# A graph kernel's front stages joined: degrees from self-loop ranks, x scaled during the edge sort; one stage split, one stage's gate banks doubled

## The chip, the cores and the metric

The kernel runs on 1 core of one Trainium2 chip. A NeuronCore has TensorE (PE, matmuls), VectorE (DVE), ScalarE (ACT), GpSimd (POOL), SyncE (SP, which here only issues DMAs) and 16 DMA engines. The metric is the device time of the whole program in microseconds (us), the median of several runs.

## The reference

Four layers of graph networks run one after the other on 50000 nodes with 128 features each. The 100000 edges come sorted by destination: 50000 random ones and one self loop per node. `deg` counts the edges of a node without its own loop.

```python
src = jnp.concatenate([_s, _d, _loop]); dst = jnp.concatenate([_d, _s, _loop])
_o = jnp.argsort(dst, stable=True); src = src[_o]; dst = dst[_o]

def gcn_layer(x, edge_index, W, b, num_nodes):        # layer 0, used twice; it adds self loops once more
    deg = jax.ops.segment_sum(jnp.ones_like(dst), dst, num_segments=num_nodes)
    dinv = jnp.where(deg > 0, jax.lax.rsqrt(deg), 0.0)
    norm = dinv[src] * dinv[dst]
    return jax.ops.segment_sum((x @ W)[src] * norm[:, None], dst, num_segments=num_nodes) + b

def sage(h, w_self, w_neigh, b):                      # layer 1, used three times
    agg = jax.ops.segment_sum(h[src], dst, num_segments=n) * inv_deg
    return h @ w_self + agg @ w_neigh + b
```

Layer 2 weighs messages by a sigmoid of source and destination and puts them through a gated recurrent unit (two gates and a candidate) with a batch norm; layer 3 is one more neighbour and self product. Between them stand residuals and layer norms.

## The kernel before, in words

Nodes lie in T = 98 groups of 512 (4 blocks of 128 partitions). The program is a chain of stages, each closed by a barrier of all engines: `sort_edges` (L301), `fold_weights` (L2110), `count_degrees` (L1000), `scale_degrees` (L1067), `scale_x` (L1128), `gcn_first` (L1167), `gcn_second`, `sage_first` (L1373), `sage_second`, `sage_third`, `attend` (L1747), two batch-norm stages and `combine`. Behind some of them stands `if_general`, a branch for inputs that don't have the expected form; it isn't taken here.

**Sort.** It takes 100000 edges as 782 columns of 128, drops the self loops and packs the other edges into 425 slots (17 for each 4 groups). VectorE works out a partition (`spot`) and a slot for every edge, builds one-hot matrices `parts` (L555, 8 columns an operation, 98 operations) and values (L547, L549), and TensorE multiplies the two to place source and destination (L413), 8 columns a round. The loads of all weights run beside it (L385).

**Degrees.** `count_degrees` builds another set of one-hots from the sorted edges (L1028, L1035) and sums them on TensorE (L1052), which gives the degree of every node; the table goes to memory. `scale_degrees` reads it back and makes 1/sqrt(deg + 1) (`dinv_n`) and 1/deg (`inv_n`), by groups of nodes and as rows in memory. `scale_x` loads x group by group (L773), multiplies it by `dinv_n` on ACT, 4 operations a group (L1150), and stores it as `t_x0` (L777).

**Stages over groups.** `over_groups` (L125) runs each engine's steps over the 98 groups with a fixed lag per step. In a stage that sums over edges, VectorE copies the indices of a group (`aim`, L642), GpSimd issues 3 to 5 indirect gathers of 128 rows (L649), VectorE builds one-hots (L677), and TensorE sums 5 or 7 pieces a group (`sum_by_feature`, L713). With `split=True` ACT first takes the rows' high part (`take_hi`, L672) and VectorE the low part (`take_lo`, L684), both in a narrower float32 form that TensorE multiplies in one pass each; without it a float32 matmul takes two passes, and the rows buffer has two rings instead of one. `gcn_first` and `sage_second` are split, `sage_first` isn't.

**attend.** Per group TensorE computes two gates into banks 3 and 4 (L1821, L1822) and the candidate's parts into banks 5 and 6 (L1824, L1825). It first waits for `opened` (ACT has read the gates of the group before) and `mixed` (VectorE has read banks 5 and 6, L1897 and L1900).

## Time and profile before

| what | us |
|---|---|
| median of 3 runs (5885.31 to 5894.61) | 5894.18 |
| the profiled execution | 5898.03 |
| its span, first to last instruction | 5896.2 |
| TensorE busy | 4786.1 (81%) |
| VectorE busy | 3866.7 (66%) |
| GpSimd busy | 2984.4 (51%) |
| ScalarE busy | 2695.8 (46%) |

How to read the rows below. A row of the table by stretch gives the stretch from the start of the span, its length, then busy time and number of instructions of PE, PEld (weight loads), DVE, ACT and POOL, the share of TensorE's clock that was granted, the busy share of the DMA engines and GB/s. A row by line gives line, engine, operation, what is written from what, the shapes (partitions x elements), the count, then busy us in all, mean ns of one, and the engine's idle time before them with what ended it. A timeline row gives start and duration in us; "x14" means that 14 instructions are merged. A float32 matmul that isn't split leaves two records, one per pass. Matmuls overlap: the distance from start to start is shorter than one's duration.

### The profile page before, as it was taken

Reading aid. Unit: us, or ns where it says so; the run is one execution under the profiler, and the core shown is the slowest. Engines: PE = TensorE matmul, PEld = TensorE weight load, DVE = VectorE, ACT = ScalarE, POOL = GpSimd, SP = SyncE. Lnnn points to the kernel's source line nnn. Section 1 sums busy time; section 2 is a strip of 40 time slices with the busy share of each in tenths; the row PEclk is TensorE's granted clock in tenths of the full one; section 3 lists DMA queues with packets and bytes.
Section 4 is the critical chain, followed back from the end, with each engine's and each line's share of the span. In section 5 each row is a group of like instructions: output and inputs, shape, how many; then the busy total and the mean of one; then the engine's idle time right before and its main releaser. Section 6 shows DMA issues by size and latency. Waiting matters only on the chain. (4 is left out here: it accounts for less than half of the span.)

```text
span 5896.2 us, 104499 instructions
## 1 busy us (share of the span) xinstructions
PE 4786.1 (81%) x27114; PEld 3751.8 (64%) x27114; DVE 3866.7 (66%) x11812; ACT 2695.8 (46%) x6502; POOL 2984.4 (51%) x2957
## 2 busy tenths in 40 slices
PE   2207999666599998999999998778699999546887
PEld 1106888555488886777777776677565666326777
DVE  9905777576666664555555554788577777786666
ACT  0074444465622222222222222677566666694455
POOL 0007776677677754343433432777555555005776
PEclk9999999777799998999999998999899999657999
DMA  1097998445467764444444443777655555595554
GB/s 31 6 326 222 274 274 270 144 147 145 144 207 226 224 208 151 149 155 146 155 149 149 155 147 102 186 199 198 185 164 155 161 159 156 178 305 158 148 151 139
DMA packets 523170, 1024.15 MB, mean 174 GB/s; under 512 B 107887, under 2 KB 115094, under 8 KB 519962
## 3 DMA queue, kind: packets, MB, share of 16 engines
q1 hardware_dynamic: 423194, 803.47, 41.2%
q0 software_dynamic: 99840, 219.14, 16.2%
q8 instruction: 52, 0.85, 0.1%
q14 instruction: 84, 0.69, 0.0%
HBM read 686.75 MB, written 335.49 MB: 173 GB/s over the span
## 5 line engine op out<-in xcount | busy, mean ns | idle before, releaser
L649 POOL DMA_INDIRECT s_rows<-t_h,s_index x416 | 526.5, 1266 | 854.9 <-DVE s_index L642 753.5
L649 POOL DMA_INDIRECT g_rows<-t_x,g_index x416 | 415.3, 998 | 594.9 <-DVE g_index L642 485.5
L649 POOL DMA_INDIRECT at_rows<-t_m,at_index x416 | 433.6, 1042 | 407.1 <-DVE at_index L642 302.4
L649 POOL DMA_INDIRECT cb_rows<-t_x,cb_index x416 | 397.9, 956 | 465.5 <-DVE cb_index L642 342.7
L713 PE MATMUL bank<-s_onehot,s_rows 128*128 128x80 f32 (+9 forms) x2344 | 475.3, 356 | 129.4 <-DMA s_rows<-t_v,s_index 93.0
L713 PEld LDWEIGHTS bank<-s_onehot,s_rows 128*128 128x128 f32 x2344 | 407.9, 203 | 190.0 <-DVE s_onehot L677 52.1
L649 POOL DMA_INDIRECT s_rows<-t_v,s_index x416 | 400.9, 964 | 211.5 <-issue 124.1
L649 POOL DMA_INDIRECT s_rows<-t_x,s_index x416 | 403.4, 970 | 179.3 <-issue 121.4
L649 POOL DMA_INDIRECT g_rows<-t_h,g_index x416 | 402.3, 967 | 172.1 <-issue 124.7
L713 PE MATMUL bank<-g_onehot,g_rows 128*128 128x80 f32 (+9 forms) x1172 | 299.2, 420 | 196.8 <-DMA g_rows<-t_h,g_index 192.2
L1599 DVE TENSOR_TENSOR s_rout<-bank,s_x 128x512 f32<-128x512 f32 x98 | 67.8, 692 | 587.2 <-PE bank L1543 587.2
L713 PEld LDWEIGHTS bank<-g_onehot,g_rows 128*128 128x128 f32 x1172 | 248.9, 243 | 251.8 <-issue 156.6
L1543 PEld LDWEIGHTS bank<-wuv_s,s_hid 128*128 128x128 f32 x3136 | 365.5, 192 | 47.4 <-issue 47.4
L677 DVE TENSOR_SCALAR s_onehot<-iota,dcol 128x224 f32<-128x224 f32 (+15 forms) x1248 | 386.0, 371 | 0.6
L1566 ACT ACTIVATE s_hid<-bank,sb_c 128x512 f32<-128x512 f32 x196 | 124.1, 684 | 569.0 <-PE bank L1531 569.0
L1531 PE MATMUL bank<-s_ht,ws_s 128*128 128x512 f32 x784 | 369.5, 594 | 0.0
L1531 PE MATMUL bank<-s_agg,wn_s 128*128 128x512 f32 x784 | 368.4, 592 | 0.0
L1543 PE MATMUL bank<-wuv_s,s_hid 128*128 128x128 f32 x3136 | 366.0, 275 | 0.9 <-DVE s_rout L1599 0.9
L713 PE MATMUL bank<-g_onehot,g_hi 128*128 128x112 f32 (+9 forms) x586 | 178.1, 340 | 180.4 <-DVE g_lo L684 171.5
L713 PE MATMUL bank<-cb_onehot,cb_rows 128*128 128x80 f32 (+9 forms) x1172 | 242.0, 360 | 91.3 <-DMA cb_rows<-t_x,cb_index 76.5
L713 PE MATMUL bank<-s_onehot,s_hi 128*128 128x80 f32 (+9 forms) x1172 | 288.4, 287 | 22.1 <-DVE s_lo L684 18.1
L713 PE MATMUL bank<-s_onehot,s_lo 128*128 128x80 f32 (+9 forms) x1172 | 285.0, 285 | 0.0
(308 smaller groups left out, 12601.2 us busy)
## 6 DMA issues: line engine op xcount, KB each, us to landing
s_scale<-inv_d SPq DMA_DIRECT2D x196, 256.0 KB
t_h<-s_hout SPq DMA_DIRECT2D x98, 512.0 KB
s_own<-t_h SPq DMA_DIRECT2D x98, 512.0 KB
t_m<-s_mout SPq DMA_DIRECT2D x98, 264.0 KB
at_own<-t_m SPq DMA_DIRECT2D x98, 264.0 KB
t_x<-sx_out SPq DMA_DIRECT2D x98, 256.0 KB
g_own<-t_x SPq DMA_DIRECT2D x98, 256.0 KB
g_scale<-dinv_d SPq DMA_DIRECT2D x98, 256.0 KB
```

The costliest lines, as they stand in the source:

```text
L649: pool.indirect_dma_start(out=self.rows[:, self.ring(q) + k, :], out_offset=None, in_=self.table[0:NPAD, :], in_offset=bass.IndirectOffset ...
L677: last = dve.tensor_scalar(self.onehot[:, k, 0:WIDE[k]], iota[:, 0:WIDE[k]], col(dcol, q.m * K + k), None, ALU.is_equal)
L713: last = pe.matmul(to[:, a:b], part[:, at, h * P:(h + 1) * P], self.onehot[:, k, off:off + b - a], start=(i + s == 0), stop=(close and i + ...
L1531: last = pe.matmul(bank[4 + o][:, :], w[:, h, o * P:(o + 1) * P], r[q.u][:, h, :], start=(k + h == 0), stop=(k + h == 2))
L1543: last = pe.matmul(bank[6 + w][:, b * D:(b + 1) * D], hid[q.u][:, h, b * P:(b + 1) * P], wuv_s[:, h, w * D:(w + 1) * D], start=(h == 0), s ...
L1566: last = act.activation(hid[q.u][:, h, :], bank[4 + h][:, :], ACT.Relu, bias=sb1_c[:, h:h + 1])
L1599: dve.tensor_tensor(rout[q.u][:, :], bank[6][:, :], xin[q.u][:, :], ALU.add)\
```

## The change

`sort_and_scale` takes the place of the sort, `fold_weights`, `count_degrees`, `scale_degrees` and `scale_x`; the last two and the slower counting stay for the general branch alone. The rank of a self loop (its place in the list less its node's number) counts the other edges up to its node. Each loop is now kept: it gets a cell of its node, and a second matmul per column puts its rank there, beside the edges'. Differences of neighbouring cells give the degrees; `below` and `corner` bring over the last cell of the partition before. The node groups are done in five pieces, each as soon as the loop has placed its ranks, and ACT scales x in place for them while the loop goes on; SP loads 11 groups ahead. The one-hots are laid out with the column index innermost (step one for VectorE, 16 elements of two bytes from column to column for TensorE's stationary operand), 16 columns an operation, from `spot` and `ramp` in bf16. In `sage_first` the rows are split. In `attend` the two gates alternate between banks (3, 4) and (2, 7), and the wait for `mixed` stands behind them.

```diff
-PACK = 8
+CELLS = 2 * BLK
+PACK = 16
+PIECE = 8 * PACK
+AHEAD = 11
+PARTS = 3
+PIECES = ((0, 6), (6, 22), (22, 42), (42, 64), (64, T))
+ROOT_AT = (None, 5, 13, 26, 55)
...
+                for t in range(AHEAD):
+                    load_rows(t)
                 sp.wait_ge(padded, 4)
                 for to, what in loads:
                     sp.dma_start(to, what, allow_slow_non_contiguous=True).then_inc(weighted, 16)
+                for t in range(T):
+                    sp.wait_ge(scaled, t + 1)
+                    sp.dma_start(group_of(t_x0[0:NPAD, :], t), xin[t % AHEAD][:, :])\
+                      .then_inc(stored[t % AHEAD], 16)
+                    if 0 <= t - 2 < T - AHEAD:
+                        sp.wait_ge(stored[(t - 2) % AHEAD], (t - 2) // AHEAD * 16 + 16)
+                        load_rows(t - 2 + AHEAD)
...
+                                parts[n % PARTS][:, :, c0 - n * PACK],
+                                value[j % 2][:, c0 - j * PIECE, :, :].rearrange("p o f -> p (o f)").bitcast(BF16)
...
+                            last = pe.matmul(
+                                bank[2 + to // 256][:, to % 256 * 2:(to % 256 + upto - to) * 2],
+                                parts[n % PARTS][:, :, c0 - n * PACK],
+                                count[j % 2][:, c0 - j * PIECE, :].bitcast(BF16)[:, (to - off) * 2:(upto - off) * 2],
+                                start=False, stop=False, skip_group_check=True)
...
+                take_root(0)
+                for t in range(T):
+                    for i, (a, b) in enumerate(PIECES):
+                        if t == a:
+                            act.wait_ge(inverted, i + 1)
+                    act.wait_ge(loaded[t % AHEAD], t // AHEAD * 16 + 16)
+                    for b in range(BLK):
+                        f = slice(b * D, (b + 1) * D)
+                        last = act.activation(xin[t % AHEAD][:, f], xin[t % AHEAD][:, f], ACT.Copy,
+                                              scale=col(dinv_n, t * BLK + b))
...
+                def lay_values(j):
+                    if j >= 2:
+                        dve.wait_ge(moved, (j - 1) * PIECE // PACK)
+                    c0, m = j * PIECE, min(PIECE, EC - j * PIECE)
+                    dve.tensor_tensor(hot[:, 0:m, :], cols(slot, c0, m, OFFS), upward(m, OFFS), ALU.is_equal)
+                    then(dve.tensor_tensor(lit[:, 0:m, :], cols(cell, c0, m, CELLS), upward(m, CELLS), ALU.is_equal))
...
+                for n in range(ROUNDS):
+                    if n * PACK % PIECE == 0:
+                        lay_values(n * PACK // PIECE)
+                    if n >= PARTS:
+                        dve.wait_ge(moved, n - PARTS + 1)
                     m = min(PACK, EC - n * PACK)
-                    dve.tensor_tensor(parts[n % 4][:, 0:m, :], cols(spot, n * PACK, m, P), ramp(m, P),
-                                      ALU.is_equal).then_inc(picked, 1)
+                    dve.tensor_tensor(parts[n % PARTS][:, :, 0:m],
+                                      spot[:, LEAD + n * PACK:LEAD + n * PACK + m].rearrange("p (o c) -> p o c", o=1)
+                                      .broadcast_to([P, P, m]), ramp[:, :, 0:m], ALU.is_equal).then_inc(picked, 1)
+                    for i in range(len(PIECES) - 1):
+                        if n == LAST_ROUND[i] + 1:
+                            add_ranks(i)
+                        if n == LAST_ROUND[i] + 2:
+                            count_nodes(i)
+                        if n == LAST_ROUND[i] + (3 if i == 0 else 5):
+                            invert_roots(i)
...
-            e = EdgeRows(ph, t_x1, D)
+            e = EdgeRows(ph, t_x1, D, split=True)
...
+            GATES = ((3, 4), (2, 7))
...
-                    if not (isinstance(q.t, int) and q.t < 1):
-                        pe.wait_ge(opened, q.t)
-                        pe.wait_ge(mixed, q.t)
+                    if not is_first(q.t):
+                        pe.wait_ge(opened, q.t - 1)
...
+                        to = bank[GATES[q.u][g]]
+                        pe.matmul(to[:, :], wih_s[:, f], agg[q.u][:, :], start=True, stop=False)
+                        last = pe.matmul(to[:, :], whh_s[:, f], xq[:, :], start=False, stop=True)
+                    last.then_inc(crossed, 1)
+                    if not (isinstance(q.t, int) and q.t < 1):
+                        pe.wait_ge(mixed, q.t)
```

`LAST_ROUND`, the round after which a piece's ranks are all placed, is 3, 11, 21, 32 and 48 of rounds 0 to 48. `add_ranks` copies a piece's cells from the bank, `count_nodes` takes the differences, `invert_roots` the reciprocal of the root. The last piece is inverted after the checks of the sorted edges, at the end of VectorE's part.

## Rows read from the trace of the kernel before

**Rows 1.** Table by stretch: us, PE, PEld, DVE, ACT, POOL, clock, DMA share, GB/s.

```profile
0.00:204.00 204.00, 43.97 (x837) 34.13 (x837) 193.41 (x215) 3.28 (x5) 4.53 (x45) 1.00 0.09 23
204.00:279.50 75.50, 16.65 (x429) 13.97 (x429) 69.56 (x35) 0.00 (x0) 0.00 (x0) 1.00 0.01 3
279.50:295.50 16.00, 1.57 (x8) 1.27 (x8) 10.51 (x17) 1.91 (x2) 0.00 (x0) 1.00 0.13 39
295.50:454.46 158.96, 0.00 (x0) 0.00 (x0) 0.00 (x0) 124.47 (x392) 0.00 (x0) 1.00 0.94 323
1613.00:2221.00 608.00, 590.31 (x3132) 524.57 (x3132) 391.87 (x906) 162.34 (x197) 403.41 (x416) 0.98 0.70 214
4215.00:5010.00 795.00, 757.99 (x2941) 471.01 (x2942) 554.04 (x1130) 522.40 (x1240) 429.84 (x413) 0.99 0.55 159
```

**Rows 2.** Costliest groups by line: the loops of the sort and of count_degrees.

```profile
L1035 DVE TENSOR_TENSOR deg_parts<-deg_spot,iota 128x2176 bf16<-128x2176 f32 x25 | 58.5, 2415 | 0.0
...
L555 DVE TENSOR_TENSOR so_parts<-so_spot,iota 128x1024 bf16<-128x1024 f32 x98 | 111.2, 1213 | 0.0
...
L413 PE MATMUL bank<-so_value,so_parts 128*128 128x28 bf16 (+4 forms) x815 | 37.4, 185 | 123.9 <-DVE so_parts L555 123.9
```

**Rows 3.** Timeline of VectorE in the sort: start, us, engine, line, operation.

```profile
11.16 0.63 DVE L464 CAST so_dst_f<-so_dst_i 128x896 f32<-128x896 int32 x1 [3.75 <-DMA so_next_i<-in_dst_dram]
...
22.62 0.59 DVE L483 TENSOR_SCALAR so_int<-so_int 128x832 int32<-128x832 int32 x1
...
24.94 1.02 DVE L487 TENSOR_TENSOR so_a<-so_a,so_rank 128x832 f32<-128x832 f32 x1
...
60.35 2.08 DVE L547 TENSOR_TENSOR so_hot<-so_slot,iota 128x1848 f32<-128x1848 f32 x1
```

**Rows 4.** Timeline of TensorE: a round of the sort, 32 float32 matmuls.

```profile
68.96 0.38 PE L413 MATMUL bank<-so_value,so_parts 128*128 128x28 bf16 x8 [0.76 <-DVE so_parts L555]
...
2908.48 3.73 PE L1543 MATMUL bank<-wuv_s,s_hid 128*128 128x128 f32 x32
```

**Rows 5.** Timeline of VectorE: end of sort, scale_degrees, start of gcn_first.

```profile
189.45 1.08 DVE L557 TENSOR_TENSOR so_scrap<-so_next_f,so_dst_f 128x896 f32<-128x896 f32 x1
...
283.74 3.35 DVE L1113 RECIPROCAL scl_b<-scl_b 98x512 f32<-98x512 f32 x1
...
454.46 0.38 DVE L642 COPY g_index<-idx 128x5 uint32<-128x5 uint32 x4 [159.07 <-PEq L254]
```

**Rows 6.** Costliest groups by line: gathers of sage_first, split of gcn_first.

```profile
L649 POOL DMA_INDIRECT s_rows<-t_x,s_index x416 | 403.4, 970 | 179.3 <-issue 121.4 <-DVE s_index L642 57.9
...
L684 DVE TENSOR_TENSOR g_lo<-g_rows,g_hi 128x640 fp32r<-128x640 f32 (+1 forms) x98 | 71.0, 724 | 99.5 <-ACT g_hi L672 99.5
```

**Rows 7.** Timeline of TensorE in sage_first: seven-piece and five-piece sum, unsplit.

```profile
1902.54 2.63 PE L713 MATMUL bank<-s_onehot,s_rows 128*128 128x112 f32 x14
...
1905.00 0.64 PE L1422 MATMUL bank<-ws_s,s_xt 128*128 128x256 f32 x2
...
1908.93 1.81 PE L713 MATMUL bank<-s_onehot,s_rows 128*128 128x80 f32 x10
...
1910.58 0.59 PE L1422 MATMUL bank<-ws_s,s_xt 128*128 128x256 f32 x2
```

**Rows 8.** Timeline of TensorE in sage_second: the same sums, split.

```profile
2911.97 0.32 PE L713 MATMUL bank<-s_onehot,s_hi 128*128 128x168 f32 x1
...
2913.11 0.32 PE L713 MATMUL bank<-s_onehot,s_hi 128*128 128x168 f32 x1
...
2925.52 0.28 PE L713 MATMUL bank<-s_onehot,s_hi 128*128 128x80 f32 x1
...
2927.24 0.26 PE L713 MATMUL bank<-s_onehot,s_hi 128*128 128x80 f32 x1
```

**Rows 9.** Timeline of TensorE in attend, one stall; and all of them by tile.

```profile
4606.26 1.10 PE L1821 MATMUL bank<-at_agg,wih_s 128*128 128x512 f32 x2 [0.42 <-DVE at_mix L1900]
...
  DVE at_mix L1900: 28.0, 50
```

More of the change, by code:

```diff
@@ L103, with first_slot, first_cell @@
 PASSED = []
+def first_slot(c):
+    return (K * c >> 5) - 3
+def first_cell(c):
+    return 4 * ((c + 20) >> 3) - 12
+PIECES = ((0, 6), (6, 22), (22, 42), (42, 64), (64, T))
+LAST_ROUND = [next(n for n in range(EC) if all(first_cell(c) >= b * BLK for c in range((n + 1) * PACK, EC)))
+              for _, b in PIECES]
+ROOT_AT = (None, 5, 13, 26, 55)
 class Turn:
@@ L326, in sort_edges @@
             here, there, back = (tmp(n, [P, COLS]) for n in ("here", "there", "back"))
[L327 to L334 removed]
+            quad, cell = tmp("quad", [P, CW]), tmp("cell", [P, CW])
@@ L335, in sort_edges @@
+            slot = e_f
+            spot, ramp = tmp("spot", [P, CW], BF16), tmp("ramp", [P, P, PACK], BF16)
+            pack = [s_t, tmp("pack", [P, CW])]
+            hot, lit = tmp("hot", [P, PIECE, OFFS]), tmp("lit", [P, PIECE, CELLS])
+            value = [tmp(f"value{u}", [P, PIECE, OFFS, 2]) for u in range(2)]
+            count = [tmp(f"count{u}", [P, PIECE, CELLS]) for u in range(2)]
+            parts = [tmp(f"parts{u}", [P, P, PACK], BF16) for u in range(PARTS)]
             filled = tmp("filled", [P, SLOTS])
+            cum = tmp("cum", [P, T + 1, BLK])
@@ L337, in sort_edges @@
+            deg, root = tmp("deg", [P, T, BLK]), tmp("root", [P, T, BLK])
+            rows = [t[:, :, :, :].rearrange("p c o f -> p (c o f)")[0:T, 0:GRP] for t in value]
+            xin = [tmp(f"x{u}", [P, GRP]) for u in range(AHEAD)]
             made, padded, got, weighted = sem("made"), sem("padded"), sem("got"), sem("weights")
             chain, cast, marked = sem("chain"), sem("cast"), sem("marked")
-            turned, kept = sem("turned"), sem("kept")
+            turned, kept, zeroed = sem("turned"), sem("kept"), sem("zeroed")
@@ L521, in _ @@
                 then(dve.tensor_tensor(c[:, :], c[:, :], b[:, :], ALU.add))
+                then(dve.tensor_tensor(quad[:, :], quad[:, :], c[:, :], ALU.subtract))
+                then(dve.tensor_tensor(quad[:, :], quad[:, :], loop[:, :], ALU.mult))
+                then(dve.tensor_tensor(c[:, :], c[:, :], quad[:, :], ALU.add))
                 then(dve.tensor_copy(i1[:, :], c[:, :]))
@@ new lines, in add_ranks @@
+                def add_ranks(i):
+                    dve.wait_ge(moved, LAST_ROUND[i] + 1)
+                    t0, t1 = PIECES[i]
+                    at = t0 * BLK % 256 * 2
+                    v = bank[2 + t0 * BLK // 256][:, at:at + (t1 - t0) * BLK * 2]\
+                        .rearrange("p (t b f) -> p t b f", b=BLK, f=2)
+                    here = cum[:, t0 + 1:t1 + 1, :]
+                    then(dve.tensor_copy(here, v[:, :, :, 1]))
+                    dve.scalar_tensor_tensor(out=here, in0=here, scalar=256.0, in1=v[:, :, :, 0],
+                                             op0=ALU.mult, op1=ALU.add).then_inc(cummed, 1)
@@ L560, in _ @@
[L560 to L561 removed]
+                sums = [t[:, :, :, :].rearrange("p c o f -> p (c o f)")[:, 0:3 * 4 * P] for t in value]
+                for n in range(4):
+                    last = dve.tensor_copy(sums[n // 3][:, n % 3 * 4 * P:(n % 3 + 1) * 4 * P], bank[4 + n][:, :])
                 then(last)
[L563 to L564 removed]
@@ L571, in _ @@
+                then(last)
                 dve.tensor_scalar(dsg[:, :], dsg[:, :], 256.0, None, ALU.subtract)
@@ L598, in _ @@
                 dve.tensor_scalar(id_own[:, :], ident[:, :], own[:, 0:1], None, ALU.mult)
+                then(dve.reciprocal(by_group(inv_n), deg[:, :, :]))
+                dve.tensor_scalar(selfinv_n[:, :], inv_n[:, :], own[:, 0:1], None, ALU.mult)
+                invert_roots(len(PIECES) - 1)
+                dve.wait_ge(inverted, len(PIECES))
+                dve.tensor_scalar(dinv2_n[:, :], dinv_n[:, :], own1[:, 0:1], None, ALU.mult)
+                dve.wait_ge(weighted, 16 * len(loads))
+                dve.tensor_tensor(brz_c[:, :], bih_c[:, 0:2], bhh_c[:, 0:2], ALU.add)
+                dve.tensor_tensor(b3_r[:, :, :], b3_r[:, :, :], b3b_r[:, :, :], ALU.add)
+                then(dve.scalar_tensor_tensor(out=wsx_s[:, :], in0=wn_s[:, :], scalar=own[:, 0:1],
+                                              in1=wsx_s[:, :], op0=ALU.mult, op1=ALU.add))
+                then(dve.tensor_tensor(wsx_s[:, :], wsx_s[:, :], ident[:, :], ALU.add))
+                dve.wait_ge(flipped, 1)
+                for i in range(2):
+                    dve.tensor_copy(rows[i], bank[2 + i][0:T, :]).then_inc(copied, 1)
     class EdgeRows:
```

306 lines of the change are left out of this document (152 added, 154 removed).

## The prediction, made before the changed kernel was run

> **What bounds the kernel now.** I read the table by stretch first, to see which engine is busy in each stage the diff touches [rows 1]. The first four stretches are the front: the sort, count_degrees, scale_degrees, scale_x, together 454.46 us. They take turns: VectorE is busy for 193.4 of 204 us and 69.6 of 75.5 while the DMA engines do nothing (shares 0.09 and 0.01), then the DMA engines are at 0.94 for 159 us while VectorE does nothing. In the costliest groups by line the sort's loop is 98 one-hot operations of 1213 ns, and TensorE idles 123.9 us for them [rows 2]. sage_first has TensorE busy 590.3 of 608 us, attend 758.0 of 795 [rows 1]. In attend the view by tile shows TensorE waiting 50 times, 28.0 us in all, for the operation that frees the gate banks [rows 9].
>
> **The front, VectorE's part of it.** count_degrees and scale_degrees go (91.5 us [rows 1]); their work enters the sort. Prices per operation: one-source float32 or integer on 832 elements 0.59 us, two-source 1.02 [rows 3]; two-source grows by (2415 - 1213)/(2176 - 1024) = 1.04 ns an element [rows 2], on 0.15 us.
> Before the loop: GpSimd's extra iota, memsets and selects (no row of their own; I put 1.6 us) and VectorE's extra conversions with the 2048-element ramp (3.6 us) lie in the 3.75 us that VectorE waits for the edges [rows 3]; about 1.4 us show. The three checks that leave the place before the transposed edges (3.3 us) give back just that, as the wait for the transposes behind them comes out; the reduce further on saves 1.0. Added in series: quad and cell (4 x 0.5 + 0.95), the clamp of columns (3 x 1.06 + 0.62), quad's three operations (3.2), two for cell (1.9). Net +10.8, so the loop starts at 60.35 + 10.8 = 71.2 [rows 3].
> The loop lays values in 7 chunks of 128 columns: 896, 1024, 896, 896 and 1024 elements, 5.6 us a chunk, 34.9 in all. The four pieces inside cost about 2.5 each, 10. Then 49 one-hots of 2048 elements. The trace has no two-source operation whose inputs are both two bytes wide. One element per 1.04 ns gives 2.28 us; reading as many bytes as the 1024-element float32 row gives 1.21. I take 1.21 (1.14 from start to start), because the layout is turned so that both inputs run with step one in two-byte elements and the one-source row shows VectorE passing two elements in the time of one [rows 3]; 2.28 stays as a rival. So 55.8 us against 111.2 [rows 2]. The loop ends at 71.2 + 34.9 + 10 + 55.8 = 171.9.
> The Trainium skill ("VectorE: DVE Perf Modes", section The perf-mode tier table) gives 1224 ns for a two-source operation on 2048 bf16 elements and 2293 ns in float32; by it the sum stays as it is, and no row here shows the first.
> Tail: the sort now ends 11.6 us after its loop (189.45 to about 201 [rows 5]); added are four checks (4.4), two copies that ACT made (1.3), the reciprocals (392 and 136 of 3.35/512 us each [rows 5], 3.5), the last piece's own 2.5 and small ones, so the last piece's scales stand at about 171.9 + 24 = 196.
>
> **The front, TensorE's part.** 1605 matmuls in 49 rounds, 33 a round, where one stage had 815 and the other 425. Eight in a round now take 0.38 us, 0.028 us from start to start [rows 4]: 0.9 us a round against VectorE's 1.14 + 5.6/8 = 1.84, hidden. But the stationary operand now has a step of 32 bytes. No row shows that. Below, 0.028; above, the float32 matmuls of 128 columns follow each other at (3.73 - 0.28)/31 = 0.111 [rows 4]. It decides from 1.84/33 = 0.056 on. I take at most twice 0.028, still hidden, worth 2 us of friction.
>
> **The front, scaling x.** It moves 98 loads and 98 stores of 256 KB; 159 us for 196 is 0.80 each [rows 1]. ACT's 392 operations are 124.5 us [rows 1] and stay below it. Eleven loads go out during the sort. Piece 0 (6 groups) is free at 76.8 + 7 x 1.14 + 2.5 = 87, piece 1 at 76.8 + 17 x 1.14 + 2 x 5.6 + 5 = 112, piece 2 at 132, piece 3 at 153. With 175 transfers left at 112 the DMA engines are the bound: group 22 comes at about 133, group 42 at 158 or later, group 64 at 200 against 196 for its piece. So the stream doesn't break, and ends at 113 + 140 = 253. SP's queue holds stores, waits for their landing and loads; at each wait four transfers (3.2 us) are queued, so it doesn't starve. The two row tables' stores, the barrier and the branch add 4, the friction 2: gcn_first starts at 259 in place of 454.5 [rows 5]. **Saved: 195.** The bias folding (3 us) is inside the tail.
>
> **sage_first, split.** A seven-piece sum takes 1905.00 - 1902.54 = 2.46 us unsplit [rows 7], 2927.24 - 2925.52 = 1.72 split; a five-piece one 1.65 against 1.14 [rows 8]. The mean gain is 0.62 us over 98 groups, 61 us of TensorE, 5.97 to 5.35 us a group. VectorE gets the low half, 0.72 us a group [rows 6], on 391.9/98 = 4.0: 4.7, still under. ACT gets about as much on 162.3/98 = 1.7 [rows 1]. But GpSimd needs (403.4 + 121.4)/98 = 5.36 us a group [rows 6] for the gathers and becomes the bound. Moreover the gather's buffer falls from two rings to one: its refill now waits for the low half of the group four earlier, behind which VectorE's index copies are queued; that has about 10 us of slack. So 5.97 to about 5.45, and 5 us lost at the ends: **saved 42**, bounds 25 (half the cap lost to the single ring) and 52 (fully at GpSimd's pace).
>
> **attend, gates.** The first two gates alternate between two pairs of banks, so TensorE does 8 matmul records (3.4 us) before it needs the bank that the row shows it waiting for [rows 9]; the candidate's wait, kept behind them, is then long met. The two new waits: blend on VectorE now waits for joined, with only group-later work behind it, and gate on ACT starts 1.7 us earlier. The row shows 28.0 us idle [rows 9]; at each stall the overlap of about 0.17 us with the matmul before is lost too, but stalls at the stage's ends stay. **Saved 29**, bounds 20 and 36. After it TensorE is late by nothing else: VectorE has 554.0 and ACT 522.4 of 795 [rows 1].
>
> **The sum.** 195 + 42 + 29 = 266. The profiled execution took 5898.03 us (span 5896.2), so 5632; the median of the runs is 3.85 below it, so **5628**.
>
> **Rivals.**
> (A) The strided stationary operand makes TensorE the bound of the sort. At 0.111 a matmul a round is 3.66 us, the loop ends at 78 + 179 = 257, less what a slack of three buffers wins back; the last piece stands at 281, 34 stores and 23 loads follow (45): gcn_first at about 326, 67 later: 5695. For it: a new step that no row covers. Against: TensorE has half its time free. The Trainium skill ("Advanced Engine Details and Errata", section SBUF Cachelines) says that each access to another 16-byte line pays a penalty, without a price, and it speaks against this layout.
> (B) The one-hots run at one element per cycle: 49 x 1.07 = 52 us more on VectorE; the last piece then stands at 248, plus 45, gcn_first at 299: 5668.
> (C) The stages behind give back little: the single ring stalls the gathers and attend finds another wait: 35 of the 71 lost, 5663.
> (D) The overlap doesn't happen, the change doing its arithmetic but not its "meanwhile": SP, ACT or the DMA order hold the stream until the last piece. Then 196 + 159 and 4: 100 later, 5728.
> (E) The other side. Weight loads don't overlap with matmuls at all at that step. With all else gained (71), the front must lose 71: gcn_first at 525, loop end at 456, (456 - 78)/1605 = 0.235 us a matmul. That is the point from which it decides; at 0.25 gcn_first starts at 78 + 401 + 24 + 45 = 548 and the kernel takes 5917. Only if each load ran in series would it come so far.
>
> **How the numbers follow.** Forecast 0.58, A 0.18, B 0.08, C 0.10, D 0.04, E 0.02. The forecast's own range is 5600 to 5650 (front 175 to 210, the others' bounds partly cancelling). The range asked for takes in A, B and C: 5600 to 5700, leaving out D, E and A's dear end. A measurement of this kernel can tell about 0.2%, 12 us. All but E are faster by far more: faster 0.97, same 0.01, slower 0.02.
>
> **What would show it.** The one-hots at 1.2 us, not 2.3; TensorE's idle in the loop put down to VectorE and not the reverse; DMA share at 0.9 from about 112 us on; gcn_first's first index copy at about 259; sage_first's gathers back to back and its stage near 566 us; in attend no wait of TensorE on the blend, stage near 766. The prediction falls if the new checks send the kernel down its general branch, or if the matmuls of the sort follow each other at over 0.056 us.

## The result, and the profile after

| | before | changed |
|---|---|---|
| median, us | 5891.73 (4 runs, 5885.31 to 5894.61) | 5641.42 (4 runs, 5636.52 to 5644.90) |
| ratio, 95% interval | | 0.9576 (0.9559 to 0.9593) |
| the profiled execution, us (span) | 5898.03 (5896.2) | 5636.52 (5634.7) |

The change takes 4.2% away. The forecast was 5628 with a range of 5600 to 5700; the measured median is 13 us above it. The sum had been made against the profiled execution and gave 5632 there; the profiled execution of the changed kernel took 5636.52.

**Where the time went.** The first thing to read is when each stage begins. These lines give for each group of gathers its first and last start. First the kernel before:

```profile
L649 POOL DMA_INDIRECT g_rows<-t_x,g_index x416: 939/947/1460, 455.2 to 1014.6; - x139
...
L649 POOL DMA_INDIRECT s_rows<-t_x,s_index x416: 939/947/1437, 1617.1 to 2171.7; - x139
L649 POOL DMA_INDIRECT s_rows<-t_h,s_index x416: 942/949/2863, 2225.4 to 3553.0; - x139
...
L649 POOL DMA_INDIRECT at_rows<-t_m,at_index x416: 939/1016/1343, 4210.3 to 5006.1; - x139
L649 POOL DMA_INDIRECT cb_rows<-t_x,cb_index x416: 941/947/1110, 5346.1 to 5869.5; - x139
```

and the changed kernel:

```profile
L840 POOL DMA_INDIRECT g_rows<-t_x,g_index x416: 939/945/1445, 281.7 to 836.6; - x139
...
L840 POOL DMA_INDIRECT s_rows<-t_x,s_index x416: 940/945/1506, 1438.7 to 1981.1; - x139
L840 POOL DMA_INDIRECT s_rows<-t_h,s_index x416: 940/947/2862, 2009.3 to 3337.7; - x139
...
L840 POOL DMA_INDIRECT at_rows<-t_m,at_index x416: 938/946/1418, 3994.5 to 4755.4; - x139
L840 POOL DMA_INDIRECT cb_rows<-t_x,cb_index x416: 938/945/1126, 5086.8 to 5608.4; - x139
```

From start to start: the front 455.2 to 281.7, 173.5 less (176 at the first index copy, 278.5 against the 454.46 of [rows 5]); the two gcn stages 1161.9 to 1157.0, 4.9 less; sage_first 608.3 to 570.6, 37.7 less; sage_second and sage_third 1984.9 to 1985.2; attend with the batch norm 1135.8 to 1092.3, 43.5 less; combine to the end of the span 550.1 to 547.9, 2.2 less. The sum is 261.5 us, the whole difference of the spans. The forecast had 195, 42 and 29, which is 266, and nothing elsewhere. So the total is closer than its parts: the front and sage_first gave 25.8 us less than was said, attend 14.5 more, and the other stages 6.8 that no term had.

**The front falls short by 19 us.** The table by stretch of the changed kernel, in the columns of [rows 1]:

```profile
88.00:97.00 9.00, 6.88 (x112) 6.82 (x111) 8.92 (x11) 7.14 (x24) 0.00 (x0) 0.50 0.53 166
97.00:117.00 20.00, 17.98 (x279) 17.83 (x278) 16.24 (x22) 0.44 (x2) 0.00 (x0) 0.50 0.17 59
117.00:131.00 14.00, 13.40 (x208) 13.30 (x207) 9.18 (x14) 9.31 (x32) 0.00 (x0) 0.50 0.72 250
131.00:146.50 15.50, 11.79 (x192) 11.73 (x191) 13.54 (x14) 15.50 (x53) 0.00 (x0) 0.50 0.94 316
146.50:161.00 14.50, 12.67 (x194) 12.52 (x193) 12.15 (x18) 0.19 (x3) 0.00 (x0) 0.50 0.55 187
161.00:185.00 24.00, 21.86 (x354) 21.80 (x354) 19.99 (x19) 23.88 (x81) 0.00 (x0) 0.50 0.83 270
...
196.00:219.30 23.30, 0.62 (x3) 0.50 (x2) 21.69 (x44) 15.51 (x49) 0.00 (x0) 0.50 0.90 294
219.30:271.50 52.20, 1.96 (x8) 1.48 (x8) 2.94 (x7) 42.38 (x136) 0.00 (x0) 0.50 0.97 328
```

Two things stand there. TensorE is busy for nearly all of each stretch inside the loop (17.98 of 20.00 us), where the forecast had it busy for half. And the DMA share, which was to be 0.9 from 112 us on, has two holes, 0.17 from 97 to 117 us (the forecast had allowed for the part before 112) and 0.55 from 146.5 to 161. The timeline of ScalarE says what each hole waits for:

```profile
88.82 7.14 ACT L535 ACTIVATE so_x<-so_x,dinv_n 128x128 f32<-128x128 f32 x24 [1.12 <-DVE dinv_n L706]
107.27 0.26 ACT L525 ACTIVATE so_root<-so_root 128x64 f32<-128x64 f32 x1 [11.31 <-DVE so_root L701]
116.81 9.49 ACT L535 ACTIVATE so_x<-so_x,dinv_n 128x128 f32<-128x128 f32 x32 [9.28 <-DVE dinv_n L706]
131.00 0.27 ACT L525 ACTIVATE so_root<-so_root 128x80 f32<-128x80 f32 x1 [4.70 <-DVE so_root L701]
131.18 15.32 ACT L535 ACTIVATE so_x<-so_x,dinv_n 128x128 f32<-128x128 f32 x52
160.81 0.28 ACT L525 ACTIVATE so_root<-so_root 128x88 f32<-128x88 f32 x1 [14.31 <-DVE so_root L701]
```

The root of piece 1 is taken at 107.27, but ScalarE then waits 9.3 us for its reciprocal: VectorE's program has it five rounds after the piece's last one, behind a 5.6 us block of values. And ScalarE's program has the root of piece 3 after group 26, so it stands for 14.3 us while the rest of piece 2 (groups 27 to 41), whose reciprocals were ready at 140.5, waits behind it. The pieces became ready at 88.8, 116.8, 140.5, 165.7 and 219.3, where the forecast had 87, 112, 132, 153 and 196.

**Why the pieces are late.** The view by tile of the one-hots, with what waited for what (us, times):

```profile
L488 PEld LDWEIGHTS bank<-so_value,so_parts x815: 140/171/309, 77.1 to 193.9; 128*128 128x128 bf16 x163
...
L714 DVE TENSOR_TENSOR so_parts<-so_spot,so_ramp x49: 1093/1220/1228, 75.8 to 188.6; 128x2048 bf16<-128x2048 bf16 x48, 128x1792 bf16<-128x1792 bf16 x1
...
  DVE so_cum L689: 14.2, 5
  DVE so_parts L714: 10.9, 16
```

The one-hots take 1.22 us, where the forecast had 1.21. But VectorE waits for TensorE 25.1 us in all, 10.9 before one-hots and 14.2 before it may read a piece's cells. TensorE's own timeline:

```profile
77.89 0.22 PE L488 MATMUL bank<-so_value,so_parts 128*128 128x28 bf16 x1
77.95 0.21 PE L498 MATMUL bank<-so_count,so_parts 128*128 128x16 bf16 x1
...
79.13 0.22 PE L488 MATMUL bank<-so_value,so_parts 128*128 128x28 bf16 x1
```

Twenty matmuls in 1.24 us: 0.062 each and not 0.028, so 33 of them take 2.05 us, more than VectorE's 1.84 a round. The prediction had named 0.056 as the point from which this decides.

### The profile page after: what moved, and what is told of

Read it like the earlier page. It is cut to its first block and busy times, and to the rows that moved or that the text cites. A ratio compares the mean times of both kernels' runs of the same rounds, so it can differ in the third digit from the quotient of the medians.

```text
span 5634.7 us, 104476 instructions
## 1 busy us (share of the span) xinstructions
PE 4777.9 (85%) x27497; PEld 3774.6 (67%) x27497; DVE 3858.3 (68%) x11909; ACT 2724.4 (48%) x6602; POOL 2987.3 (53%) x2962
## 5 line engine op out<-in xcount | busy, mean ns | idle before, releaser
L840 POOL DMA_INDIRECT s_rows<-t_x,s_index x416 | 416.9, 1002 | 152.8 <-issue 117.3
L840 POOL DMA_INDIRECT g_rows<-t_h,g_index x416 | 402.8, 968 | 171.9 <-issue 123.1
L904 PE MATMUL bank<-s_onehot,s_hi 128*128 128x80 f32 (+9 forms) x1758 | 438.1, 289 | 42.4 <-DVE s_lo L875 26.6
L904 PE MATMUL bank<-s_onehot,s_lo 128*128 128x80 f32 (+9 forms) x1758 | 432.2, 286 | 0.0
L868 DVE TENSOR_SCALAR s_onehot<-iota,dcol 128x276 fp32r<-128x276 f32 (+15 forms) x1248 | 387.2, 373 | 0.5
L904 PEld LDWEIGHTS bank<-s_onehot,s_hi 128*128 128x128 f32 x1758 | 341.9, 194 | 49.0 <-issue 47.7
L904 PE MATMUL bank<-s_onehot,s_rows 128*128 128x80 f32 (+9 forms) x1172 | 255.7, 374 | 116.4 <-DMA s_rows<-t_v,s_index 106.8
L863 ACT ACTIVATE s_hi<-s_rows 128x640 fp32r<-128x640 f32 (+1 forms) x196 | 172.6, 880 | 371.2 <-DMA s_rows<-t_x,s_index 351.3
L904 PEld LDWEIGHTS bank<-s_onehot,s_lo 128*128 128x128 f32 x1758 | 342.6, 195 | 0.3 <-issue 0.2
```

The lines of the kernel that those rows point to most:

```text
L840: pool.indirect_dma_start(out=self.rows[:, self.ring(q) + k, :], out_offset=None, in_=self.table[0:NPAD, :], in_offset=bass.IndirectOffset ...
L863: act.activation(self.hi[:, a:b, :], self.rows[:, a:b, :], ACT.Copy).then_inc(self.split, 1)
L868: last = dve.tensor_scalar(self.onehot[:, k, 0:WIDE[k]], iota[:, 0:WIDE[k]], col(dcol, q.m * K + k), None, ALU.is_equal)
L904: last = pe.matmul(to[:, a:b], part[:, at, h * P:(h + 1) * P], self.onehot[:, k, off:off + b - a], start=(i + s == 0), stop=(close and i + ...
```

## Experiments

Twelve kernels in three groups. The first four went to a chip on which the gathers take longer whatever the kernel: there the kernel before took 6835.36 us (19 runs), and the gathers of gcn_first stretched over 756 us in place of 559 (read in `split_only`, whose gcn_first is that of the kernel before). The front, which holds no gather, took the same time as elsewhere: the first gather of `split_only` comes at 453.1 and that of `gates_only` at 451.8, against 455.2. So these four are read by their front stages, and by comparison with each other, and three of them were run again in the second and third group, where the kernel before took 5884.91 and 5888.28 us.

**1. The overlap undone** (`no_meanwhile`).

```diff
-                take_root(0)
+                for i in range(len(PIECES)):
+                    take_root(i)
+                act.wait_ge(inverted, len(PIECES))
                 for t in range(T):
-                    for i, (a, b) in enumerate(PIECES):
-                        if t == a:
-                            act.wait_ge(inverted, i + 1)
...
-                    for i in range(1, len(PIECES)):
-                        if t == ROOT_AT[i]:
-                            take_root(i)
```

> The changed kernel, but ScalarE takes all five roots first and waits for all five pieces before it scales the first group, so that nothing is stored while the loop runs. Theory: the last piece stands at 219 us as before, 98 stores and 87 loads of 256 KB follow at 0.80 us each, 148 us, so the stream ends at 367 in place of 271: 96 us more, about 5737. Rival: the stream of x slows the loop itself (its transfers or ScalarE's accesses reach the matmuls of 0.062 us or the one-hots); then the loop ends clearly before 194 us without it, the matmuls follow each other at less than 0.062, and the cost is under 80 us.

6774.64 us, a ratio of 0.9892 (0.9857 to 0.9928) to the kernel before on the same chip. The first gather came at 377.8 and not 281.7: 96.1 us, as the theory had it. The changed kernel itself was not run on this chip, so the whole times can't be compared. The row of ScalarE's first scale and the table by stretch of this kernel:

```profile
219.43 26.96 ACT L534 ACTIVATE so_x<-so_x,dinv_n 128x128 f32<-128x128 f32 x92 [21.95 <-DVE dinv_n L702]
```

```profile
77.00:194.00 117.00, 103.78 (x1618) 103.14 (x1619) 91.04 (x113) 1.03 (x4) 0.00 (x0) 1.00 0.01 2
219.00:367.00 148.00, 1.95 (x8) 1.48 (x8) 3.33 (x8) 122.55 (x392) 0.00 (x0) 1.00 0.94 320
```

With no transfer (share 0.01) and hardly an operation of ScalarE beside it, the loop still ends at 194.2 and VectorE still waits 25.2 us for TensorE. So the stream of x slows neither engine, and the 0.062 us isn't contention with it. It isn't the clock either: TensorE's granted clock was 1.00 here, its full level of 2.4 GHz, and 0.50 (1.2 GHz) in the same loop of the changed kernel's profile, with the same interval.

**2. The order of roots and reciprocals** (`roots_moved`, `roots_again`).

```diff
-ROOT_AT = (None, 5, 13, 26, 55)
+ROOT_AT = (None, 5, 18, 36, 62)
...
-                        if n == LAST_ROUND[i] + (3 if i == 0 else 5):
+                        if n == LAST_ROUND[i] + (3 if i < 2 else 5):
                             invert_roots(i)
...
                 then(dve.tensor_reduce(seen[:, 0:1], scrap_, AX_X, ALU.add))
+                invert_roots(len(PIECES) - 1)
...
-                invert_roots(len(PIECES) - 1)
```

The last piece is thus inverted ahead of the copies of the sorted edges and no longer at the end.

> The changed kernel with the same arithmetic, but three places moved: ScalarE takes the roots of pieces 2, 3 and 4 after groups 18, 36 and 62 (not 13, 26, 55), VectorE inverts piece 1 three rounds after its last round and not five (that is ahead of a 5.6 us block of values), and the last piece in front of the copies of the sorted edges. In the changed kernel the DMA engines are busy for 0.17 of 97 to 117 us, when piece 1 is waited for, and for 0.55 of 146.5 to 161 us, when ScalarE stands 14.3 us at piece 3's root with 15 scalable groups behind it. Theory 1, the stream of x bounds the front and its breaks cost what the forecast missed: piece 1 at 110, then 175 transfers of 0.80 us, the first index copy of gcn_first near 260 and not 278.5, about 18 us less: 5623. Theory 2, the pace of TensorE's strided matmuls bounds the front: the loop still ends at 194, the last piece is at 204 and the gain is at most the 4 us that ScalarE waited for it: 5637.

> The changed kernel with the roots of pieces 2 to 4 taken after groups 18, 36 and 62, piece 1 inverted three rounds after its last and the last piece ahead of the copies of the edges, once more at the usual pace of the gathers. Theory: the first gather at 265.5 in place of 281.7 as in the earlier run of it, 16 us less, 5625. Rival: the stages behind give it back: 5636 or more.

`roots_moved`: 6643.31 us, 0.9715 (0.9681 to 0.9750), first gather at 265.5. `roots_again`: 5625.99 us, 0.9554 (0.9541 to 0.9567), first gather at 268.4. The loop ends at 194.4 in both, so TensorE's pace is untouched, and yet the front is 13 to 16 us shorter. The table of `roots_again`:

```profile
97.00:109.00 12.00, 11.43 (x175) 11.34 (x175) 8.36 (x14) 0.28 (x2) 0.00 (x0) 1.00 0.26 98
109.00:131.00 22.00, 19.69 (x306) 19.53 (x306) 16.81 (x20) 15.33 (x52) 0.00 (x0) 1.00 0.86 284
131.00:141.00 10.00, 6.27 (x102) 6.21 (x102) 9.89 (x13) 3.90 (x14) 0.00 (x0) 1.00 0.71 221
141.00:161.00 20.00, 18.19 (x283) 18.04 (x282) 15.78 (x20) 17.60 (x60) 0.00 (x0) 1.00 0.87 281
161.00:250.00 89.00, 35.11 (x522) 34.26 (x520) 48.98 (x81) 70.36 (x225) 0.00 (x0) 1.00 0.94 312
```

Piece 1 is now scaled from 109.0 on, and the hole of 0.55 is gone. The breaks of the stream set the end of the front, not the end of the loop: theory 1. It gave 18 us and 5623; measured were 13 to 16 and 5626. The three moves were made together, so their shares aren't known. That of the last piece is at most about 4 us, by estimate, since ScalarE waited 4.14 us for it in the changed kernel.

**3. The step of the stationary operand.** Five layouts of the same one-hots. In `step16`, `step4` and `roots_step8` a run of RUN columns (8, 2, 4) lies innermost; the last also has the order of experiment 2, and so has `roots_rows`.

```diff
-            parts = [tmp(f"parts{u}", [P, P, PACK], BF16) for u in range(PARTS)]
+            parts = [tmp(f"parts{u}", [P, PACK // RUN, P, RUN], BF16) for u in range(PARTS)]
...
-                                parts[n % PARTS][:, :, c0 - n * PACK],
+                                parts[n % PARTS][:, (c0 - n * PACK) // RUN, :, c0 % RUN],
...
```

VectorE's operation goes through one block of RUN columns after the other. Where the columns of a round don't fill whole runs, it is split in two; only the last round does that.

`dense` writes each column in one piece, `parts` being [P, PACK, P], while VectorE reads as before:

```diff
-                    dve.tensor_tensor(parts[n % PARTS][:, :, 0:m],
+                    dve.tensor_tensor(parts[n % PARTS][:, 0:m, :].rearrange("p c q -> p q c"),
```

`roots_rows` has that tile too, but goes through it in its own order:

```diff
+                    dve.tensor_tensor(parts[n % PARTS][:, 0:m, :],
+                                      spot[:, LEAD + n * PACK:LEAD + n * PACK + m].rearrange("p (c o) -> p c o", o=1)
+                                      .broadcast_to([P, m, P]), ramp[:, 0:m, :], ALU.is_equal).then_inc(picked, 1)
```

> The changed kernel, its one-hots laid as two halves of 8 columns, so that TensorE's stationary operand has a step of 16 bytes in place of 32 and VectorE's inner runs are 8 elements. The matmuls follow each other at 0.062 us with a step of 32 bytes, at granted clocks of 0.50 and of 1.00 alike, and at 0.028 without a step. Theory 1, the load of the operand pays for the distance between its elements: an interval between 0.028 and 0.062, near 0.045. Theory 2, any step of more than one element costs the same: 0.062 again, loop end 194. VectorE: 1.22 us if a run of 8 elements is long enough for it, up to 2.3 if not.

> As the kernel with the step of 16 bytes, but eight parts of 2 columns: a step of 4 bytes. Theory 1 (the distance is paid): an interval of 0.028 to 0.035 us. Theory 2 (any step costs the same): 0.062. For VectorE runs of 2 elements: 1.22 us if only the step within the run counts, near 2.3 if the runs have to be longer; in the second case the loop ends near 71 + 35 + 10 + 49 x 2.27 = 227, 33 us later than with the layout of the change, and the first index copy of gcn_first comes up to 33 us later.

> The changed kernel with the stationary operand dense (128 elements of two bytes one behind the other); VectorE reads as before with step one and writes with a step of 256 bytes. TensorE: 0.028 us from matmul to matmul, as in the sort of the kernel before; 33 of them take 0.9 us. VectorE: 1.22 us if what it reads sets its speed, then the loop ends near 172 as was forecast, 22 us before that of the change, but the roots taken late keep part of that: the first index copy of gcn_first 5 to 15 us before 278.5. Rival: the written step sets the speed, 2.2 to 2.3 us, the loop ends near 227, and the kernel is 20 to 30 us behind the changed one.

> As roots_again, with the one-hots in four parts of 4 columns: a step of 8 bytes for TensorE's stationary operand and runs of 4 elements for VectorE. Matmuls follow each other at 0.062 us with a step of 32 or 16 bytes and at 0.028 with 4 or 2; VectorE takes 1.22 us with runs of 16 and 8 and 2.02 with runs of 2. Theory 1: the load is slow from a step of 16 bytes on, so 0.028 here, and VectorE at 1.3 to 1.5 us sets the pace: the loop ends at 172 to 185 and the last piece 10 to 20 us earlier. Theory 2: any step above 4 bytes is slow: 0.062, loop end 192 to 194. In both the stream of x is bound by the DMA engines from piece 1 on, so that the kernel gains at most 5 us over roots_again.

> As roots_again, with one-hots laid by column as in the kernel before (TensorE's stationary operand dense, 0.028 us a matmul) but both inputs in bf16: the place of the edge stands still along the inner run of 128 elements, the ramp steps by one. This is the layout whose price the forecast's rival B assumed. Theory 1: an input that stands still keeps VectorE at one element in 1.07 ns, 2.2 to 2.3 us an operation; the loop ends near 71 + 35 + 10 + 49 x 2.27 = 227 and the first gather comes 15 to 30 us after that of roots_again. Theory 2: only the width of the elements counts, 1.22 us; then neither engine is slowed, the loop ends near 175, and this is the best of the layouts, up to 5 us ahead of roots_again.

The weight loads and the one-hots in the view by tile (min/median/max ns), first of `step16`, then `step4`, `roots_step8`, `dense`, `roots_rows`:

```profile
L489 PEld LDWEIGHTS bank<-so_value,so_parts x815: 142/171/308, 77.2 to 192.3; 128*128 128x128 bf16 x163
...
L719 DVE TENSOR_TENSOR so_parts<-so_spot,so_ramp x50: 553/1220/1226, 75.9 to 187.7; 128x2048 bf16<-128x2048 bf16 x48, 128x1024 bf16<-128x1024 bf16 x1, 128x768 bf16<-128x768 bf16 x1
```

```profile
L489 PEld LDWEIGHTS bank<-so_value,so_parts x815: 103/104/291, 78.0 to 206.1; 128*128 128x128 bf16 x163
...
L719 DVE TENSOR_TENSOR so_parts<-so_spot,so_ramp x49: 1767/2021/2064, 75.9 to 203.5; 128x2048 bf16<-128x2048 bf16 x48, 128x1792 bf16<-128x1792 bf16 x1
```

```profile
L489 PEld LDWEIGHTS bank<-so_value,so_parts x815: 110/118/291, 77.2 to 169.7; 128*128 128x128 bf16 x163
...
L719 DVE TENSOR_TENSOR so_parts<-so_spot,so_ramp x50: 379/1218/1228, 75.9 to 168.3; 128x2048 bf16<-128x2048 bf16 x48, 128x1536 bf16<-128x1536 bf16 x1, 128x256 bf16<-128x256 bf16 x1
```

```profile
L714 DVE TENSOR_TENSOR so_parts<-so_spot,so_ramp x49: 8111/9479/9494, 75.9 to 545.9; 128x2048 bf16<-128x2048 bf16 x48, 128x1792 bf16<-128x1792 bf16 x1
```

```profile
L714 DVE TENSOR_TENSOR so_parts<-so_spot,so_ramp x49: 2021/2282/2287, 75.9 to 216.2; 128x2048 bf16<-128x2048 bf16 x48, 128x1792 bf16<-128x1792 bf16 x1
```

With the intervals of the matmuls (from start to start over at least eight, by their timelines):

| kernel | step, bytes | weight load, ns | interval, us | one-hot, us | loop ends | first gather | median, us | ratio (95%) |
|---|---|---|---|---|---|---|---|---|
| changed | 32 | 171 | 0.062 | 1.22 | 194.0 | 281.7 | 5641.42 | 0.9576 (0.9559 to 0.9593) |
| `step16` | 16 | 171 | 0.060 | 1.22 | 192.4 | 278.6 | 5636.40 | 0.9579 (0.9563 to 0.9595) |
| `step4` | 4 | 104 | 0.027 | 2.02 | 206.2 | 292.6 | 5648.79 | 0.9601 (0.9585 to 0.9617) |
| `dense` | 2 | 104 | 0.027 | 9.48 | 554.9 | 636.0 | 5993.60 | 1.0185 (1.0168 to 1.0202) |
| `roots_again` | 32 | 169 | 0.062 | 1.22 | 194.4 | 268.4 | 5625.99 | 0.9554 (0.9541 to 0.9567) |
| `roots_step8` | 8 | 118 | 0.033 | 1.22 | 169.8 | 257.2 | 5614.35 | 0.9532 (0.9519 to 0.9545) |
| `roots_rows` | 2 | 104 | 0.027 | 2.28 | 219.0 | 284.2 | 5644.43 | 0.9587 (0.9574 to 0.9600) |

The step sets TensorE's pace: two kernels with one step have one interval, whatever VectorE takes. It doesn't do so in proportion: from 4 to 8 bytes the interval grows by 0.006 us, from 8 to 16 by 0.027, from 16 to 32 by 0.002. For `step16` that is theory 2, for `step4` theory 1 on TensorE, and VectorE near the dearer of the two values (2.02 against 2.3, so the loop ends at 206 and not 227); for `roots_step8` theory 1, with VectorE better than hoped (1.22, not 1.3 to 1.5). What was expected there of the whole was wrong: "at most 5 us" over `roots_again`, measured 11.6, since the scales of piece 1 start at 101.94 in place of 108.98, 7 us sooner (the first row is of `roots_again`, the second of `roots_step8`):

```profile
108.98 15.35 ACT L535 ACTIVATE so_x<-so_x,dinv_n 128x128 f32<-128x128 f32 x52 [1.34 <-DVE dinv_n L706]
```

```profile
101.94 15.34 ACT L536 ACTIVATE so_x<-so_x,dinv_n 128x128 f32<-128x128 f32 x52 [1.34 <-DVE dinv_n L707]
```

`roots_rows` is theory 1: an input that stands still keeps VectorE at 1.1 ns an element although both are bf16. For `dense` both theories fell. VectorE takes 9.48 us for 2048 elements, 4.6 ns each, and the kernel is 352 us behind the changed one.

`roots_step8` has the lowest median of the study. The 95% interval of its ratio lies wholly below that of the change; it overlaps that of `roots_again` by 0.0004, while every one of its runs (5605.93 to 5616.28) is faster than every one of `roots_again` (5619.54 to 5629.36).

**4. sage_first's split alone** (`split_only`, `split_again`; the line of the change, with the ACT and VectorE steps that belong to a split).

```diff
-            e = EdgeRows(ph, t_x1, D)
+            e = EdgeRows(ph, t_x1, D, split=True)
...
-                over_groups(act, [(2, turn), (6, relu)])
+                over_groups(act, [(2, turn), (6, relu), (0, lambda q: e.take_hi(act, q))])
...
-                e.on_vector(dve, [(3, mean), (5, bias), (0, lambda q: e.prepare(dve, q))])
+                e.on_vector(dve, [(3, mean), (5, bias), (0, lambda q: e.prepare_split(dve, q))])
```

> The kernel before with sage_first's rows split and nothing else. The forecast priced this at 42 us (bounds 25 and 52), a stage near 566 us. In the trace of the changed kernel the time from sage_first's first gather to that of the stage behind is 570.6 us against 608.3: 37.7 less. Theory: the split alone does this, so 5891.7 - 38 = 5854 and the same two gather times 570 to 572 us apart. Rival: part of the 38 us comes from what the other edits left behind (the order in which the gathers start after the shorter front): then less than 30 us, above 5862.

> The kernel before with sage_first's rows split alone, once more, to be read in the same job as a kernel before whose gathers come at the pace of the first comparison (in the last job that kernel took 6835 us, its gathers stretched over 756 us in gcn_first in place of 559, and the split made sage_first 31 us longer). Theory: where GpSimd's gathers are 1.3 us apart the stage is bound by TensorE, and the split saves 38 us (stage 570.6 against 608.3). Rival: the single ring of buffers eats the gain here too, and the 38 us came from the other edits: then under 15 us. If the gathers are slow again, the stage gets longer again, by 20 to 35 us.

`split_again`: 5854.94 us, 0.9951 (0.9935 to 0.9968), 30 us less than before. In its trace the gathers of sage_first and of the stage behind start 572.3 us apart (608.3 before): 36 us in the stage, which the median bears out within its interval of 19 to 38. `split_only`, where gathers are slow: 6864.80 us, 1.0035 (1.0010 to 1.0060), 29 us more. The stage of `split_only`, then that of `gates_only`, which is unsplit, on the same chip:

```profile
1952.90:2738.40 785.50, 617.33 (x3132) 532.34 (x3132) 456.89 (x1005) 212.46 (x294) 408.28 (x417) 0.85 0.53 166
```

```profile
1948.00:2702.70 754.70, 645.12 (x3132) 550.51 (x3132) 389.38 (x907) 159.25 (x196) 401.44 (x417) 0.91 0.55 173
```

TensorE has 28 us less to do and the stage is 31 us longer. The two other kernels with the split that ran on this chip have it at 777.8 (`no_meanwhile`) and 770.5 us (`roots_moved`) from first gather to first gather, 23 and 16 us longer. Once rows come late, TensorE's time is worth nothing, and something of the split costs. The single ring of row buffers is the likely one; no run had the split with two rings, so that stays open.

**5. attend's gates alone** (`gates_only`, `gates_again`: the gate banks and the moved wait, that is the last part of the diff with the semaphore `joined` that belongs to it, in the kernel before).

```diff
-                    if not (isinstance(q.t, int) and q.t < 1):
-                        pe.wait_ge(opened, q.t)
-                        pe.wait_ge(mixed, q.t)
+                    if not is_first(q.t):
+                        pe.wait_ge(opened, q.t - 1)
...
+                    last.then_inc(crossed, 1)
+                    if not (isinstance(q.t, int) and q.t < 1):
+                        pe.wait_ge(mixed, q.t)
```

> The kernel before with attend's two pairs of gate banks and the moved waits, nothing else. The forecast priced this at 29 us (bounds 20 and 36). In the trace of the changed kernel attend's sums run from first to last start in 787.1 us against 824.2 before (37 less), and attend with the batch-norm stages behind takes 43.5 us less. Theory 1: the gates are worth 37 us in attend, so 5855. Theory 2: the gates give the forecast 29 us, 5863, and the rest is from elsewhere. Either way TensorE no longer waits for the blend on VectorE (25.1 us before, 0.8 in the changed kernel).

> The kernel before with attend's gate banks alone, once more, at the usual pace of the gathers. In the trace of the changed kernel attend and the batch-norm stages behind take 43.5 us less than before, from the first gather of attend to that of combine 1092.3 against 1135.8. Theory: the two pairs of banks are all of it; each of the 50 stalls also lost about 0.2 us of overlap between matmuls that the idle time of 28.0 us doesn't show (the step from one group of matmuls to the next is 1.52 us at a stall and 0.90 without one, where 0.42 was shown idle), which gives 28 + 10 in attend, and 5 at its end. So 1092 and about 5843. Rival: only the forecast 29 us: 1107 and 5857.

`gates_only`: 6803.85 us, 0.9957 (0.9934 to 0.9980). `gates_again`: 5839.65 us, 0.9917 (0.9902 to 0.9933), 49 us less; attend with the batch norm takes 1091.5 us in it against 1135.8, 44.3 less, so this edit is all of it. The waits of TensorE in attend (us in all, times, longest), first before, then in the changed kernel, show the stall gone:

```profile
PE bank L1821 <- DVE at_mix L1900: 25.1, 49, 4.9
PE bank L713 <- ACT at_mine L1850: 23.1, 1, 23.1
```

```profile
PE bank L904 <- ACT at_mine L1979: 23.2, 1, 23.2
PE bank L1953 <- DVE at_mix L2031: 0.8, 1, 0.8
```

(The 28.0 us in 50 of [rows 9] come from the view by tile; the matmuls' own waits are these 25.1 in 49.) The operation waited for, L1900, ends VectorE's reading of the candidate's banks 5 and 6; the prediction's first paragraph takes it for the one that frees the gates' banks. So the wait that was moved behind the gates is the one that stood in the way. Whether moving it alone would have done, without the second pair of banks, no run tells.

## Why the prediction was right, and where it was not

**Right: the whole.** Faster by 4.2% for the reason given. Undoing the overlap costs 96 us (rival D said 100), the split alone gives 36 in its stage and attend's edit alone 44. The other 77 us of the front's 173.5 come with the stages that are gone and the cheaper one-hots; no kernel had these alone, and they are read from the traces. That 261.5 us came where 266 were forecast is in part luck: the front and sage_first gave 25.8 less, and attend and the stages without a term made up for 21.3 of it. By the prediction's own sign it was to fall, since the matmuls of the sort do follow each other at over 0.056 us. The total held because the pace is paid only in part: with the roots moved it is worth 11 us (experiment 3), well inside the range.

**Right in the front:** the loop starts when forecast (first one-hot 75.8, with the first block of values from 70.2); the one-hots at 1.22 us; the tail of 24 us from the loop's end to the last piece (194.3 to 219.3 is 25); 0.80 us a transfer (148 us for the 185 of `no_meanwhile`). The Trainium skill ("VectorE: DVE Perf Modes", section The perf-mode tier table) agrees here: its 1224 ns for the two-source operation on bf16 stand beside the measured 1220. Its 2293 ns are for float32; `roots_rows`, in bf16 with an input that stands still, measured 2282.

**The step that failed: "Above 0.028, below 0.111 ... I take at most twice 0.028, still hidden".** It is 0.062, over the 0.056 named as the point of decision. That put the loop's end at 194 and not 171.9. With a step of 8 bytes the interval is 0.033 and the loop ends at 169.8: the forecast's sum for VectorE was right to 2 us, and its one wrong term was TensorE's. The choice was made from the wrong side: 0.056 was the threshold, and twice 0.028 sat on it by construction, so it should have carried more than rival A's chance. The Trainium skill ("Advanced Engine Details and Errata", section SBUF Cachelines) names a penalty for each access to another 16-byte line. The measured cliff between a step of 8 and one of 16 bytes agrees with it. The price, 0.027 us a matmul for a stationary operand of 128 columns, comes from these runs.

**The second step that failed: "So the stream doesn't break".** It had been weighed against the DMA engines and not against ScalarE's own order. A root that stands between two scales holds every scale behind it: 14.3 us at piece 3, where the DMA share fell to 0.55. The reciprocal put five rounds late isn't part of the miss, since the forecast's 112 for piece 1 counts its 17 rounds and two blocks of values; putting it earlier is a gain over the forecast. Moving the three places gave 13 to 16 us back with TensorE untouched. How the 19 us that the front fell short divide between the two steps isn't measured: no kernel had both engines fast and the roots in the change's order (`step4` had TensorE fast, but VectorE at 2.02 us). With both mended the first gather is at 257.2, 24.5 us sooner than in the changed kernel; its index copy lies some 3 us before it (278.5 and 281.7 in the changed kernel), so near 254 where the forecast said 259.

**Rival A was half right:** right engine and right cause, at a little over half its 0.111 us, and its price with the roots moved is the 11 us between `roots_again` and `roots_step8`, not 67, since it only counts where a piece is waited for. **Rival B** (one element a cycle) didn't come true; `roots_rows` priced it at 16 us of front over `roots_again`, not 40, because TensorE had been the slower one by then. **Rival C** didn't happen at this pace of gathers. On the chip with slow gathers sage_first did lose 16 to 31 us by the split; whether by the ring, as C had it, isn't shown.

**sage_first: 42 forecast, 38 seen** (36 alone). GpSimd is at 5.45 us a group in the split stage (416.9 busy and 117.3 issuing over 98 groups), the period that was forecast; the stage took 570.6 us where 566 was said.

**attend: 29 forecast, 43.5 seen, above the bound of 36.** The mechanism held and the term was mis-sized. The text had the overlap of 0.17 us that each stall loses and then left it out for "stalls at the stage's ends". At the stall of [rows 9] the step from one group of matmuls to the next takes 1.52 us and without a stall 0.92 on the mean, so 0.60 is lost where 0.42 is shown as idle. The row ahead of it in that timeline is the group before:

```profile
4604.74 1.10 PE L1807 MATMUL bank<-id_own,at_mine 128*128 128x128 f32 x8
```

The matmuls behind are late too: from this group to the second gate's first matmul (L1822) it is 2.54 us on the mean in 48 groups with the stall and 1.79 in 48 without, 36 us in all, of which 25 are shown as idle. In the trace the sums of attend run 37.1 us shorter, and from the last one to combine's first gather it is 6.4 us less. The last was in no term, and its cause is open. From first to last gather the stage takes 760.9 us (795.8 before), where near 766 was said.

## What to carry to other kernels

A layout that suits VectorE can cost TensorE: 16-element runs of bf16 were no faster to build than 4-element ones, and the step of 32 bytes they left more than doubled the time from matmul to matmul, where 8 bytes were nearly free. When an engine does two jobs in one program order, write down the order, not only the sum of the times: ask of each wait what that doesn't need it stands behind it. And idle time is not all that a stall costs in a stream of matmuls; take the step from start to start with and without the stall.

## What the runs showed of the hardware beyond what was expected

- A bf16 stationary operand of 128 columns loads in 104 ns at steps of 2 and 4 bytes, 118 at 8, 171 at 16 and at 32. The cliff is between 8 and 16.
- VectorE wrote bf16 at a step of 256 bytes at 4.6 ns an element (9479 ns for 2048), four times as slow as with an input that stands still (2282 ns), and kept its fast form down to runs of 4 elements (1218 ns), but not at 2 (2021).
- The same front had a granted clock of 0.50 (the level of 1.2 GHz) in some profiles and of 1.00 in others. In the changed kernel's it was 1.00 until 20 us and 0.50 from 20 to 70 us, where TensorE was busy for 1.29 us; in `no_meanwhile`, as idle there, it stayed at 1.00. The 0.062 us, the 310 ns of a float32 weight load in the loop and the loop's end were the same in both.
- One chip was 16% slower than the others on the same kernel (6835 us against 5888), in stages that wait for gathers (gcn_first's 756 us against 559), and there one of the three parts of the change turned into a loss.
